# A graph layer on one core: 31 of its 1563 edge chunks are fetched row by row by SyncE instead of by GpSimd's gather

## The reference, cut to what matters

```
seg  = dst * R + edge_type                       # R = 65
sums = segment_sum(x[src], seg).reshape(N, R, 128)
cnt  = segment_sum(ones,   seg).reshape(N, R, 1)
conv = einsum('nri,rio->no', sums / max(cnt, 1), W_rel)
h    = conv + x @ W_root + bias + x @ W_res + b_res
out  = layernorm(x + relu(batchnorm(h)))
```

## Time and profile before

| what | value |
|---|---|
| median of 3 runs | 2020.98 us |
| the profiled execution: its time, its span | 2019.47 us, 2017.8 us |
| TensorE matmul busy, weight load busy | 1903.8 us (94%), 1767.9 us (88%) |
| GpSimd busy | 1480.4 us (73%) |
| VectorE busy, ScalarE busy | 1417.4 us (70%), 884.4 us (44%) |
| TensorE clock granted | 0.998 |
| DMA engines, mean busy share in the loop | 0.49 |

### The profile page before, as it was taken

How to read it: one execution, slowest core, us unless ns; L and a number is a source line. 1 busy time by engine, 2 the same in 40 slices (tenths; PEclk the granted TensorE clock), 3 DMA queues, 4 the chain that set the end, 5 groups by cost and what they waited for, 6 DMA issues and landing times.

```text
span 2017.8 us, 38034 instructions
## 1 busy us (share of the span) xinstructions
PE 1903.8 (94%) x13396; PEld 1767.9 (88%) x13396; DVE 1417.4 (70%) x2424; ACT 884.4 (44%) x1637; POOL 1480.4 (73%) x1582
## 2 busy tenths in 40 slices
PE   6999999999999999999999999999999999999998
PEld 3899988889889889889889888988988988988987
DVE  7887786686676677677667668668667667766756
ACT  4544444434434444444444444444443444444444
POOL 7777777777777777777777777777777777777760
PEclk9999999999999999999999999999999999999999
DMA  8744544544544544454454454454454444444444
GB/s 289 210 107 108 113 107 107 112 107 106 112 107 106 113 106 108 105 112 107 106 112 106 108 112 107 106 114 105 108 112 108 105 109 105 108 105 108 106 100 123
DMA packets 243101, 232.81 MB, mean 115 GB/s; under 512 B 27253, under 2 KB 237599, under 8 KB 242271
## 3 DMA queue, kind: packets, MB, share of 16 engines
q0 software_dynamic: 221264, 202.74, 45.7%
q1 hardware_dynamic: 21647, 27.60, 4.4%
HBM read 217.43 MB, written 12.80 MB: 114 GB/s over the span
## 4 chain that ended last, share of the span: by engine, by line
PE 73%; DMA 18%; POOL 4%; issue 3%; DVE 2%; SPq 0%; ACT 0%; DVEq 0%; ACTq 0%; POOLq 0%
PE tb L700 32%; PE ps L664 31%; DMA xg<-xtab,srcT 17%; POOL xg L557 4%; PE ps L668 4%; PE tb L592 4%; DMA cols<-in_L_gnn_beta_dram 0%; DVE same L976 0%; DVE lst L1234 0%; PE tb L642 0%; PE ps L778 0%; DVE agg L1258 0%; DVE onehot L1043 0%; ACT agg L892 0%; PE ps L791 0%
## 5 line engine op out<-in xcount | busy, mean ns | idle before, releaser
L557 POOL DMA_INDIRECT xg<-xtab,srcT x1529 | 1439.5, 941 | 468.1 <-issue 247.1
L1043 DVE TENSOR_SCALAR onehot<-iota,segT,vT 128x456 fp32r<-128x456 f32 x1563 | 1112.8, 742 | 331.2 <-PE ps L668 326.6
L806 ACT ACTIVATE agg<-ps 128x390 f32 (+1 forms) x1563 | 842.4, 539 | 1085.4 <-PE ps L668 1036.1
L664 PE MATMUL ps<-onehot,xg 128*128 128x390 f32 x3058 | 1106.0, 429 | 86.4 <-DMA xg<-xtab,srcT 84.7
L700 PE MATMUL tb<-agg,wsb 128*128 128x138 f32 (+1 forms) x6370 | 1094.1, 298 | 1.3 <-issue 1.3
L700 PEld LDWEIGHTS tb<-agg,wsb 128*128 128x128 f32 x6370 | 840.6, 190 | 2.4 <-issue 1.4
L664 PEld LDWEIGHTS ps<-onehot,xg 128*128 128x128 f32 x3058 | 573.3, 189 | 166.6 <-DMA xg<-xtab,srcT 135.0
L668 PE MATMUL ps<-onehot,xg 128*128 128x66 f32 x2962 | 577.8, 195 | 0.0
L668 PEld LDWEIGHTS ps<-onehot,xg 128*128 128x128 f32 x2962 | 564.4, 191 | 2.8
L976 DVE SCALAR_TENSOR_TENSOR same<-ps,rel 128x1088 bf16<-128x1088 f32 (+3 forms) x96 | 145.4, 1514 | 0.0
L592 PE MATMUL tb<-same,identb 128*128 128x512 bf16 x416 | 108.7, 384 | 9.4 <-DVE same L976 9.3
(11 more groups left out here) (137 smaller groups left out, 366.1 us busy)
## 6 DMA issues: line engine op xcount, KB each, us to landing
xg<-xtab,srcT POOLq DMA_INDIRECT x1529, 2.8
xtab<-agg SPq DMA_DIRECT2D x4, 1536.0 KB
hinit<-H SPq DMA_DIRECT2D x1, 3125.0 KB, 20.2
agg<-in_x_dram SPq DMA_DIRECT2D x4, 768.0 KB, 7.7
out_dram<-agg SPq DMA_DIRECT2D x6, 448.0 KB, 3.0
dsth<-in_dst_dram SPq DMA_DIRECT2D x23, 64.0 KB
eth<-in_edge_type_dram SPq DMA_DIRECT2D x23, 64.0 KB
srcr<-in_src_dram SPq DMA_DIRECT2D x12, 64.0 KB, 1.9
```

The lines of the kernel that those rows point to most:

```text
L557: pool.indirect_dma_start(out=xg[i % RING][:], out_offset=None, in_=xtab.bitcast(F32R), in_offset=bass.IndirectOffsetOnAxis(ap=srcT[t % 2] ...
L664: return nc.tensor.matmul(bank[:, 0:w], rows_in_sbuf(c, part), marks(c, 0, w), start=(part == 0), stop=(part == n_own - 1 and part >= n_ca ...
L806: nc.scalar.activation(agg_group(g)[:, :, bass.ds(off, n)], ps[c % NRB][:, 0:n * R].rearrange("f (n r) -> f r n", r=R), ACT.Copy).then_inc ...
L1043: nc.vector.tensor_scalar(onehot[o][:].rearrange("p (a b) -> p a b", a=3), iota3[:, :, 0:IW], segT[t % 2][:, k:k + 1], vT[t % 2][:, k:k + ...
```

## The change

Chunks 105, 153, 201, ..., 1545 (31 chunks, `by_sp`) leave GpSimd's loop. For them VectorE makes byte offsets (source node x 1024) once, after the marks of chunk 12; two small loads bring their source indices to `spsrc`, one chunk per partition. SyncE then loads 16 offsets at a time into registers and issues one DMA of 1024 bytes for each of the 128 rows, with the register as the byte offset in the table, into one of two new buffers `xsp`. The fetch of the a-th such chunk waits for the sums of the (a-2)-th. TensorE waits for 128 x 16 counts of `sp_in`. GpSimd's ring now goes on over the chunks that are left, and `load_rows(t)` stands between the fetches.

```diff
+SP_FIRST = 105
+SP_STEP = 48
+SP_REGS = 16
+SP_OFFS = 12
...
+    ROWB = 4 * 2 * F
+    tab_bytes = xtab.rearrange("n f -> (n f)").bitcast(U8)
...
+    by_sp = list(range(SP_FIRST, NCH, SP_STEP))
+    NSP = len(by_sp)
+    in_ring = [c for c in range(FX, NCH) if c not in by_sp]
+    ring_of = {c: i for i, c in enumerate(in_ring)}
...
+        spsrc = sb("spsrc", [NSP, P], I32)
+        xsp = [sb(f"xsp{s}", [P, 2 * F], F32R) for s in range(2)]
...
         def rows_in_sbuf(c, part):
-            return xg[(c - FX) % RING][:, part * F:(part + 1) * F]
+            buf = xg[ring_of[c] % RING] if c in ring_of else xsp[by_sp.index(c) % 2]
+            return buf[:, part * F:(part + 1) * F]
...
+            whole = SP_STEP * (NSP - 1)
+            sp.dma_start(spsrc[0:NSP - 1, :], src[SP_FIRST * P:(SP_FIRST + whole) * P].rearrange(
+                "(a k e) -> a k e", k=SP_STEP, e=P)[:, 0, :]).then_inc(sp_src, 16)
+            sp.dma_start(spsrc[NSP - 1:NSP, :], src[by_sp[-1] * P:(by_sp[-1] + 1) * P].rearrange("(a e) -> a e", a=1)).then_inc(sp_src, 16)
             sp.wait_ge(raw_free, 1)
             load_rows(1)
...
-            for t in range(2, NTL):
-                sp.wait_ge(raw_free, t)
-                load_rows(t)
+            def fetch_chunk(a):
+                s = a % 2
+                if a == 0:
+                    sp.wait_ge(sp_off, 1)
+                    sp.wait_ge(tab_out, 16 * 3)
+                    sp.wait_ge(tab_rest, 16 * 3)
+                if a >= 2:
+                    sp.wait_ge(agg_ps, by_sp[a - 2] + 2)
+                for e in range(0, P, SP_REGS):
+                    starts = registers(spsrc[a:a + 1, e:e + SP_REGS], ENG.SP, (N - 1) * ROWB)
+                    for k in range(SP_REGS):
+                        sp.dma_start(xsp[s].bitcast(U8)[e + k:e + k + 1, :],
+                                     tab_bytes[bass.ds(starts[k], ROWB)].rearrange("(a b) -> a b", a=1)
+                                     ).then_inc(sp_in[s], 16)
+
+            t = 2
+            for a in range(NSP):
+                while t < NTL and by_sp[a] >= (t - 2) * TC + DVE_SEG + 2 * SP_STEP + 12:
+                    sp.wait_ge(raw_free, t)
+                    load_rows(t)
+                    t += 1
+                fetch_chunk(a)
...
-            for c in range(FX, NCH):
-                t, k, i = c // TC, c % TC, c - FX
+            for i, c in enumerate(in_ring):
+                t, k = c // TC, c % TC
...
-                pool.wait_ge(agg_ps, c - RING + 2 if i >= RING else FIRST_SUMS + i * CATCH_UP // RING)
+                pool.wait_ge(agg_ps, in_ring[i - RING] + 2 if i >= RING else FIRST_SUMS + i * CATCH_UP // RING)
...
             def aggregate(c):
                 if c < FX:
                     pe.wait_ge(first_in[c], 16)
+                elif c in ring_of:
+                    pe.wait_ge(gath[ring_of[c] % RING], 16 * (ring_of[c] // RING + 1))
                 else:
-                    pe.wait_ge(gath[(c - FX) % RING], 16 * ((c - FX) // RING + 1))
+                    a = by_sp.index(c)
+                    pe.wait_ge(sp_in[a % 2], 16 * P * (a // 2 + 1))
...
                 one_hot(c)
+                if c == SP_OFFS:
+                    dve.wait_ge(sp_src, 32)
+                    nc.vector.tensor_scalar(spsrc[:], spsrc[:], float(ROWB), None, ALU.mult).then_inc(sp_off, 1)
```

More of the change, by code:

```diff
@@ L11 @@
 I32 = mybir.dt.int32
+U8 = mybir.dt.uint8
 ALU = mybir.AluOpType
@@ L119, in pair_len @@
         return min(GC, NCH - p * GC)
+    by_sp = list(range(SP_FIRST, NCH, SP_STEP))
+    NSP = len(by_sp)
+    assert SP_FIRST > FX + RING and NCH - by_sp[-1] > 0 and P % SP_REGS == 0
+    in_ring = [c for c in range(FX, NCH) if c not in by_sp]
+    ring_of = {c: i for i, c in enumerate(in_ring)}
     def row_loads(t):
@@ L281, in gnn @@
         agg_ps = sem("agg_ps")
+        sp_src = sem("sp_src")
+        sp_off = sem("sp_off")
+        sp_in = [sem(f"sp_in{s}") for s in range(2)]
         evac = sem("evac")
@@ L462, in _ @@
             sp.dma_start(hinit, H[:, 0:N]).then_inc(hinit_out, 16)
-            for t in range(2, NTL):
-                sp.wait_ge(raw_free, t)
-                load_rows(t)
+            def fetch_chunk(a):
[19 more added lines that the diff above has]
+                fetch_chunk(a)
+            assert t == NTL
             def fast():
```

## The result

The median after the change is 1982.12 us (1980.49 to 1986.46, 4 runs), against 2020.16 us before (2018.92 to 2023.32, 4 runs). The ratio is 0.9818, 95% interval 0.9805 to 0.983: 38.0 us less (34 to 39 by the interval), where the sum said 38.5. The profiled execution is the slowest of the four (1986.46 us, span 1984.7 us), so in the trace only 33.1 us are gone.

The account below looks back on a forecast made before the run. GpSimd's gather issue, 1.243 us each, was taken as the bound: 31 gathers fewer save 38.5 us, span 2017.8 to 1979.3 us, execution 1981.0, median 1982.5, stated as 1983 us (1.9% faster). Range 1977 to 2125 us.

Parts of the forecast that it names:

- the sum: Whole kernel: 31 gathers fewer at 1.243 us save 38.5 us, all on the path; waits and TensorE charged nothing.
- GpSimd's issue is the bound: Gather loop: 0.94 us busy plus 0.30 us idle, 1.243 us per gather, sets the pace; TensorE follows.
- The saving stays whole: TensorE's sums: 151.6 us needed per tile against GpSimd's 155.8, so all 38.5 us are kept; 46 us of standing stays.
- rival 2: TensorE's sums: TensorE takes over before 38.5 us are saved; half the gain, 2002 us; chance 0.06.
- X = 46.4 us: SyncE's fetch of one moved chunk: 128 row DMAs at 0.34 us plus 2.9 us for eight register loads.
- The upper bound, 5.3 us: SyncE's eight register loads per chunk at 0.66 us each, priced from a load of one value on SyncE.
- The limit X <= 57.8 us: SyncE's fetch per chunk: up to 57.8 us, 0.429 us per row, keeps up; above it SyncE sets the pace.
- the three rows of 256 bytes: SyncE's one-row loads in the old trace: 0.34, 0.29 and 0.25 us, 0.38 to 0.30 with gap; basis of 0.34.
- A one-row DMA with a register offset: SyncE's row loop: 0.34 us per row forecast; feared 0.436 + 0.04 us, making SyncE the bound, 2174 us, chance 0.28.
- Waits added: SyncE's wait for sums, VectorE's at chunk 12, two more loads: cost 0; VectorE's 2 us without cover.
- Rival 3: GpSimd's gathers get longer beside SyncE's stream: 0.026 us each takes the gain away, 0.07 gives 2087 us; chance 0.04.
- theory B: Expectation in the first experiment: SyncE's stream lengthens each gather about 4 ns, eating 6 us of 38.5; without it 1976 us.

Follow-up runs that it names:

- step96: The changed kernel with every 96th chunk (16) moved to SyncE instead of every 48th (31): 2000.65 us against 2019.95 for the kernel before, ratio 0.9904.
- no_stream: The changed kernel without SyncE's row fetches, the 31 chunks summed from buffers filled once: 2394.23 us against 2430.67 for the kernel before, ratio 0.985.
- no_stream_b: Second run of the kernel of no_stream, without SyncE's row fetches: 2388.41 us against 2427.0 for the kernel before, ratio 0.9849.
- after_again: The changed kernel, unchanged, measured once more on another chip: 2449.64 us against 2427.31 for the kernel before, ratio 1.0085.
- the first experiment: The changed kernel with SyncE's row fetches left out, run twice (no_stream, no_stream_b): ratios 0.985 and 0.9849 against the kernel before.
- before_again: The kernel before the change, unchanged, measured and profiled once more on another chip: 2429.6 us, span 2427.9 us.

## Why the prediction was right, step by step

- **GpSimd's issue is the bound, 1.243 us per gather.** Shown where the kernel before takes 2020 us, and only there. 16, 31 and 92 gathers fewer gave 19.3, 38.0 and 110.5 us, 1.20 to 1.23 us each, the first two with the stream and the last without, so no price of the stream is seen there. With 92 the interval is 1.16 to 1.23 us for each, so 1.243 is just outside, and some 4 us of that saving are missing without a cause that was looked for.
- **The saving stays whole, since TensorE has room.** Shown, and there is more of it than I counted. "The rest of TensorE's 84.7 us of standing stays as 46 us" was mis-sized: 69.1 us stayed. I took the whole saving out of the waits; in the trace 17.8 us came out of the busy time (1903.8 to 1886.0) and 15.6 out of the waits, together 33.4, the span's 33.1. For the same reason rival 2 was judged by a wrong measure: 94% busy is no sign that TensorE is near its limit, and it did not take over at three times the saving.
- **SyncE's fetch, X = 46.4 us.** The mechanism was right, the sum 6.3 us short. The rows were as estimated, 0.322 us against 0.34 us. In them is a register operation per row that I had said is not needed (MOVE, 29 ns); the DMA itself is shorter than I took it for. The term that was mis-sized is the register load: eight of 1.26 us, 10.1 us, against 2.9 us. I had taken the price of a load of 4 values on ScalarE, 0.36 us with its gap; 16 values cost four times as much. The upper bound, 5.3 us, from one value on SyncE, did not hold it either: the error was to count loads where values count.
- **The limit X <= 57.8 us.** The fetch of 52.7 us is within it, and the 5.1 us that are left for each fetch are seen as SyncE's 4.8 us of waiting. The gain stood on 5.1 us per chunk, not on 11.4. That it stood is partly luck: with the register loads as they are and the rows at 0.38 us, the dearest that the three rows of 256 bytes gave, X would have been 128 x 0.38 + 10.1 = 58.7 us, past the limit. What happens past the limit was shown with 37 chunks, on the other chips.
- **A one-row DMA with a register offset.** 228 ns, below all three rows for one row of 256 bytes. The rule of the Trainium skill (DMA: Bandwidth & Descriptors, "Why a DMA increments its semaphore by 16 and not by 1") made me fear 0.436 us, what 15 rows cost. The section has no price for the missing counts; the price was my reading of it. The trace shows none for one row. SyncE's DMA queue has 29630 packets after the change and 21647 before, two more for each of the 3968 row DMAs: one with the row and one of 4 bytes. So a row DMA brings one count of its 16 with it, and however the other 15 are made, they do not hold SyncE for longer.
- **Waits added.** None cost what could be seen: no wait of VectorE or TensorE for `spsrc` or `xsp` in the trace.
- **Rival 3, gathers that get longer beside the stream.** Their mean rose from 941 to 946 ns in the profiled execution, which by the busy times (0.9415 and 0.9455 us) and 1498 gathers is 6 us, about what the profiled execution lacks to 38 us. It does not come from the stream: where the stream is left out the mean is 943 ns (the group of L595 above), and with half of it 942 ns (`step96`, group below). On the other chips it is 944 ns without the stream (`no_stream`, `no_stream_b`), 944 with it (`after_again`) and 943 in the kernel before. So a few ns vary from run to run, which is against theory B of the first experiment. The 26 ns at which this rival would decide are far off.

```profile
L601 POOL DMA_INDIRECT xg<-xtab,srcT x1513 | 1425.3, 942 | 463.3 <-issue 255.1
```

What the prediction did not have at all is that the price of the stream depends on the chip, or on what differs between chips. Where the kernel before takes 2427 us, it is 61 us and the change loses. That the result was measured where the kernel takes 2020 us is luck. Had it been measured on one of the others, the forecast would have failed, and not by any of its rivals: SyncE kept up, TensorE did not wait for its rows, and gathers were not longer. Its first step would have failed too, since GpSimd is not the bound there. What stays open is what the stands are that, with the lower clock behind them, make the kernel 400 us longer there, and which property of the stream adds to them. The equal worth of the removal in both, 38 us, is measured but not explained: there TensorE does not stand for gathers.

## What to carry to other kernels

An idle time that is the same before each instruction of an engine, whatever releaser is named, was here the cost of issuing. Such an engine can be the bound at 73% busy, and a saving there is counted as instructions times spacing. The engine that follows it can hide part of its slack in its busy time, as TensorE did here, so read its room from a run in which the pacing engine has less to do, not from the busy share. Check the bound again where the kernel's own time differs: on the other chips the same kernel had TensorE for its bound, and a saving of the right size there proved nothing of the mechanism. When work is moved to an idle engine, price the helpers by the number of values that they handle, and compare the sum with the limit: here 6 us per chunk, from a term that looked small, took more than half of the margin.

## What the runs showed of the hardware

- A register load on SyncE took 1.26 us for 16 values; on the other chips 1.14 us for 16 and 2.08 us for 32. A single value took 0.61 us.
- A DMA of one row of 1 KB, its place given by a register, holds SyncE for 228 ns, plus 29 ns for a MOVE; 3968 of them started 0.322 us apart within a fetch.
- GpSimd issued an indirect gather of 128 rows every 1.243 to 1.246 us in the median, and no two started less than 1.238 us apart, in any of the traces, with stream or without.
- TensorE's busy time is not the work of its matmuls: the same 13396 were busy 1903.8 us and, with less waiting for gathers, 1844.0 us.
- The same kernel took 2020 us in the run of the forecast and on one more chip, and 2427 to 2431 us on each of three others. In the trace of one of those (`before_again`) 1.3 us of "issue" waits at L700 had become 165.8 us, the granted clock had fallen from 0.998 to 0.935, and the matmuls' busy time had grown from 1903.8 to 2055.7 us. A stream of one-row DMAs that costs next to nothing at 2020 us costs 61 us there.
